# Counting edges in two spans of 24 targets for each group, where four chunks shared a span of 40

## The reference

```python
dst = jnp.minimum((1024 * jax.random.uniform(key, (32768,)) ** 2.0).astype(jnp.int32), 8191)
...
x = layernorm(x + L0(x))   # D^-1/2 (A + A^T > 0, + I) D^-1/2 (x @ W) + b
x = layernorm(x + L1(x))   # three GCN layers, edges counted with their multiplicity
x = layernorm(x + L2(x))   # attention with the mask A
x = layernorm(x + L3(x))   # two GCN layers with a ReLU between
```

## Time and profile before

| | us |
|---|---|
| median of 3 runs (lowest, highest) | 600.25 (598.95, 600.39) |
| the profiled execution, its own time | 599.57 |
| its span | 597.7 |
| TensorE busy | 582.0 |
| VectorE busy | 298.0 |
| ScalarE busy | 174.7 |
| counting stage, first to last counting matmul | 16.2 to 125.5 |

### The profile page before, as it was taken

How to read it: one execution, slowest core, us unless ns; L and a number is a source line. 1 busy time by engine, 2 the same in 40 slices (tenths; PEclk the granted TensorE clock), 3 DMA queues, 4 the chain that set the end, 5 groups by cost and what they waited for, 6 DMA issues and landing times.

```text
span 597.7 us, 6522 instructions
## 1 busy us (share of the span) xinstructions
PE 582.0 (97%) x2137; PEld 347.7 (58%) x2137; DVE 298.0 (50%) x826; ACT 174.7 (29%) x360; POOL 102.1 (17%) x112
## 2 busy tenths in 40 slices
PE   4999999999999999999999999999999999999996
PEld 3555655555787854788854544444444487458742
DVE  5999889946677314134584101333334440450065
ACT  2898688736102221011011111111114102110200
POOL 3000000006412700000142002023333170000012
PEclk9999999999999999999999999999999999999998
DMA  8514000000000000000040000000000000000012
GB/s 301 210 42 171 1 0 2 2 1 1 2 2 3 0 1 0 1 0 1 0 158 1 0 0 1 0 0 1 0 0 2 2 1 0 0 1 0 1 53 88
DMA packets 7904, 15.66 MB, mean 26 GB/s; under 512 B 432, under 2 KB 448, under 8 KB 7872
## 3 DMA queue, kind: packets, MB, share of 16 engines
q1 hardware_dynamic: 7872, 15.21, 7.0%
HBM read 13.12 MB, written 2.10 MB: 25 GB/s over the span
## 4 chain that ended last, share of the span: by engine, by line
PE 96%; DVE 1%; issue 1%; ACT 1%; DMA 0%; POOLq 0%; POOL 0%; SPq 0%; ACTq 0%
PE bank L632 18%; PE bank L587 15%; PE bank L570 15%; PE bank L737 9%; PE bank L757 9%; PE bank L499 6%; PE bank L473 5%; PE bank L725 5%; PE bank L481 2%; PE bank L444 2%; PE bank L477 2%; PE bank L463 2%; PE bank L747 1%; PE bank L436 1%; PE bank L640 1%
## 5 line engine op out<-in xcount | busy, mean ns | idle before, releaser
L384 POOL TENSOR_TENSOR rstd<-veps,mhalf 128x1 f32<-128x1 f32 x32 | 23.9, 748 | 307.0 <-DVE veps L1062 307.0
L983 DVE TENSOR_SCALAR hot_key<-col_key,keyed 128x320 bf16<-128x320 int16 x256 | 65.1, 296 | 0.1
L737 PE MATMUL bank<-xt,tt 128*128 128x512 f32 x128 | 56.1, 592 | 0.0
L757 PE MATMUL bank<-vv,probt 128*128 128x512 f32 x128 | 56.1, 592 | 0.0
L632 PE MATMUL bank<-v_sb,gt 128*128 128x512 f32 x128 | 55.3, 592 | 0.0
L587 PE MATMUL bank<-adj,y_hi 128*128 128x512 f32 x128 | 51.3, 401 | 0.0
L587 PE MATMUL bank<-adj,y_lo 128*128 128x512 f32 x128 | 50.5, 395 | 0.0
L499 PEld LDWEIGHTS bank<-hot_key,hot_lo 128*128 128x128 bf16 x256 | 25.2, 98 | 38.9 <-DVE hot_key L983 16.6
L499 PE MATMUL bank<-hot_key,hot_lo 128*128 128x320 bf16 x256 | 45.8, 302 | 0.0
L1069 DVE SCALAR_TENSOR_TENSOR xs<-bank,dinv,xs 128x512 f32<-128x512 f32 x24 | 17.7, 746 | 54.0 <-PE bank L632 38.3
L820 ACT ACTIVATE apart<-col_lo,edge_key 128x128 bf16<-128x128 int16 x128 | 43.8, 391 | 0.0
(11 more groups left out here) (178 smaller groups left out, 950.7 us busy)
## 6 DMA issues: line engine op xcount, KB each, us to landing
w_sb<-in_L_gnn_W_dram SPq DMA_DIRECT2D x3, 1024.0 KB, 5.4
xs<-in_x_dram SPq DMA_DIRECT2D x2, 1024.0 KB, 7.9
v_sb<-in_L_gnn_W_dram SPq DMA_DIRECT2D x2, 1024.0 KB, 6.7
out_dram<-xs SPq DMA_DIRECT2D x8, 256.0 KB, 2.0
w_sb<-in_L_gnn_weight_dram SPq DMA_DIRECT2D x1, 1024.0 KB, 8.2
wq_sb<-in_L_gnn_Wq_dram SPq DMA_DIRECT2D x1, 1024.0 KB, 12.1
wk_sb<-in_L_gnn_Wk_dram SPq DMA_DIRECT2D x1, 1024.0 KB, 13.8
wv_sb<-in_L_gnn_Wv_dram SPq DMA_DIRECT2D x1, 1024.0 KB, 7.5
```

Of the source, the lines that this page charges most:

```text
L737: mm = pe.matmul(bank[:, 2 * (i % 2) + c, :], tt[:, k, i * P:(i + 1) * P], xt[:, k, c * D:(c + 1) * D], start=k == 0, stop=k == FB - 1)
L757: mm = pe.matmul(bank[:, 6 + i % 2, :], probt[:, i % 2, j, :], vv[:, j, :], start=j == 0, stop=j == NB - 1)
L983: V.tensor_scalar(hot_key[:, slot * CPG + c, :], col_key[:], keyed[:, 0, bass.ds(g + c * G, 1)], None, ALU.is_equal).then_inc(hot_set, 1)
```

## The change

- WIN goes from 40 to 24, and each pair of chunks (PAIR = 2) gets a span of its own. A group has two spans, side by side in its bank. Both `hot_key` and the counting matmul go from 320 to 192 columns.
- The tables of limits, first targets and rounds are by span, so twice as long.
- A group's bank is added in two adds of 8 x 24 instead of one of 8 x 40. The first comes ahead of the one-hots of three groups later, the second behind them, with a semaphore of its own (`span_added`) between the two. Before, the one-hots came ahead of the one add.
- Places are loaded for four groups at a time, one load for each span.
- SHARE goes from 1300 to 1500 columns a group.
- The low parts of `ya` come one block earlier among the `sym`.

```diff
 CPG = 4
-WIN = 40
+WIN = 24
+PAIR = 2
 BY_DVE = 2
 EARLY = 24 * 128
-SHARE = 1300
+SHARE = 1500
...
             def chunk(at_hot, at_bank, c):
-                return pe.matmul(bank[:, at_bank, 0:KEYS], hot_lo[:, at_hot, :], hot_key[:, at_hot, :],
-                                 start=c == 0, stop=c == CPG - 1)
+                span = slice(c // PAIR * KEYS, (c // PAIR + 1) * KEYS)
+                return pe.matmul(bank[:, at_bank, span], hot_lo[:, at_hot, :], hot_key[:, at_hot, :],
+                                 start=c % PAIR == 0, stop=c % PAIR == PAIR - 1)
...
-            V.tensor_reduce(group_lim[:, 0:1], edge_rows[:, 0, :], AX.X, ALU.min)
-            then(V.tensor_reduce(group_lim[:, 1:2], edge_rows[:, 0, :], AX.X, ALU.max))
-            then(V.tensor_tensor(group_lim[:, 2:3], group_lim[:, 1:2], group_lim[:, 0:1], ALU.subtract))
+            by_span = edge_rows[:, 0, :].rearrange("g (s e) -> g s e", s=SPANS)
+            V.tensor_reduce(group_lim[:, 0, :], by_span, AX.X, ALU.min)
+            then(V.tensor_reduce(group_lim[:, 1, :], by_span, AX.X, ALU.max))
+            then(V.tensor_tensor(group_lim[:, 2, :], group_lim[:, 1, :], group_lim[:, 0, :], ALU.subtract))
...
-            def windows_at(g):
-
-                _, values = nc.values_load_multi_w_load_instructions(
-                    base_at[0:1, bass.ds(g, BODY)], engines=[mybir.EngineType.DVE], min_val=0, max_val=N,
-                    skip_runtime_bounds_check_because="the table's entries are clamped to [0, N] when it is written")
-                return values
-
-            def add_window(at_dst, seen, slot):
+            def places_at(g):
+
+                loaded = []
+                for n in range(SPANS):
+                    _, values = nc.values_load_multi_w_load_instructions(
+                        base_at[0:1, bass.ds(g + n * G, HALF)], engines=[mybir.EngineType.DVE], min_val=0, max_val=N,
+                        skip_runtime_bounds_check_because="the table's entries are clamped to [0, N] when it is written")
+                    loaded.append(values)
+                return list(zip(*loaded))
+
+            def add_span(at_dst, slot, n):
+
+                return V.tensor_tensor(count[:, :, bass.ds(at_dst, WIN)],
+                                       bank[:, slot, n * KEYS:(n + 1) * KEYS].rearrange("p (h d) -> p h d", h=NB),
+                                       count[:, :, bass.ds(at_dst, WIN)], ALU.add)
+
+            def one_group(g, at_dst, seen, slot, ahead):
 
                 dve.wait_ge(win_summed, seen + 1)
                 dve.wait_ge(win_added, seen + 2)
-                V.tensor_tensor(count[:, :, bass.ds(at_dst, WIN)],
-                                bank[:, slot, 0:KEYS].rearrange("p (h d) -> p h d", h=NB),
-                                count[:, :, bass.ds(at_dst, WIN)], ALU.add).then_inc(win_added, 1)
+                add_span(at_dst[0], slot, 0).then_inc(span_added, 1)
+                if ahead is not None:
+                    one_hots(ahead, (slot + AHEAD) % SLOTS)
+                dve.wait_ge(span_added, seen + 1)
+                add_span(at_dst[1], slot, 1).then_inc(win_added, 1)
...
-                    places = windows_at(q * BODY)
                     for n in range(BODY):
-                        one_hots(q * BODY + (n + AHEAD), (n + AHEAD) % SLOTS)
-                        add_window(places[n], r * G + q * BODY + n, n % SLOTS)
...
+                        if n % HALF == 0:
+                            places = places_at(q * BODY + n)
+                        one_group(q * BODY + n, places[n % HALF], r * G + q * BODY + n, n % SLOTS, q * BODY + (n + AHEAD))
...
-                if 3 <= h < 3 + HALF:
-                    low(h - 3, ya, xw[:, h - 3, :], dinv[:, 0, h - 3:h - 2])
+                if 2 <= h < 2 + HALF:
+                    low(h - 2, ya, xw[:, h - 2, :], dinv[:, 0, h - 2:h - 1])
```

More of the change, by code:

```diff
@@ L50, in gnn_kernel @@
     ROUNDS = (N + WIN - 1) // WIN
+    SPANS = CPG // PAIR
     KEYS = NB * WIN
     SCALE = float(D) ** -0.5
-    assert D == 512 and NB == 2 * HALF and G % BODY == 0 and BODY % SLOTS == 0 and KEYS <= 512 and G <= P
+    assert D == 512 and NB == 2 * HALF and G % BODY == 0 and BODY % SLOTS == 0 and SPANS * KEYS <= 512 and SPANS * G <= P
     with ExitStack() as ctx:
@@ L156, in gnn_kernel @@
         bqb = sb("bqb", [P, FB], F32)
[L157 to L160, removed]
+        group_lim = sb("group_lim", [G, 3, SPANS], F32)
+        group_dia = sb("group_dia", [G, 2 * SPANS, G], F32)
+        group_row = sb("group_row", [P, 2, SPANS * G], F32)
+        base_at = sb("base_at", [1, SPANS * G], I32)
         rounds_f = sb("rounds_f", [P, ROUNDS + 2], F32)
@@ L197, in gnn_kernel @@
         win_added = sem("win_added")
+        span_added = sem("span_added")
         counted = sem("counted")
@@ L487, in _ @@
             pe.wait_ge(rows_set, 1)
-            pe.matmul(bank[:, 0, 0:2 * G], ones[0:G, :], group_dia[:].rearrange("g a b -> g (a b)"),
+            pe.matmul(bank[:, 0, 0:2 * SPANS * G], ones[0:G, :], group_dia[:].rearrange("g a b -> g (a b)"),
                       start=True, stop=True).then_inc(rows_turned, 1)
@@ L947, in _ @@
             dve.wait_ge(edges_in, 32)
-            V.tensor_reduce(group_lim[:, 0:1], edge_rows[:, 0, :], AX.X, ALU.min)
-            then(V.tensor_reduce(group_lim[:, 1:2], edge_rows[:, 0, :], AX.X, ALU.max))
-            then(V.tensor_tensor(group_lim[:, 2:3], group_lim[:, 1:2], group_lim[:, 0:1], ALU.subtract))
+            by_span = edge_rows[:, 0, :].rearrange("g (s e) -> g s e", s=SPANS)
+            V.tensor_reduce(group_lim[:, 0, :], by_span, AX.X, ALU.min)
+            then(V.tensor_reduce(group_lim[:, 1, :], by_span, AX.X, ALU.max))
+            then(V.tensor_tensor(group_lim[:, 2, :], group_lim[:, 1, :], group_lim[:, 0, :], ALU.subtract))
             dve.wait_ge(const_set, 1)
-            V.tensor_scalar(group_dia[:, 0, :], ident[0:G, 0:G], group_lim[:, 0:1], None, ALU.mult)
-            V.tensor_scalar(group_dia[:, 1, :], ident[0:G, 0:G], group_lim[:, 2:3], None,
-                            ALU.mult).then_inc(rows_set, 1)
+            for n in range(2 * SPANS):
+                ins = V.tensor_scalar(group_dia[:, n, :], ident[0:G, 0:G],
+                                      group_lim[:, 2 * (n // SPANS), n % SPANS:n % SPANS + 1], None, ALU.mult)
+            ins.then_inc(rows_set, 1)
             V.tensor_scalar(bits[:, 0, :], edge_rows[:, 1, :], P - 1, None, ALU.bitwise_and)
@@ L958, in _ @@
             V.tensor_scalar(key_rows[:, 1, :], bits[:, 1, :], float(WIN), None, ALU.mult)
-            V.tensor_scalar(key_rows[:, 2, :], edge_rows[:, 0, :], group_lim[:, 0:1], None,
-                            ALU.subtract).then_inc(rows_set, 1)
+            for n in range(SPANS):
+                of_span = slice(n * PAIR * P, (n + 1) * PAIR * P)
+                ins = V.tensor_scalar(key_rows[:, 2, of_span], edge_rows[:, 0, of_span], group_lim[:, 0, n:n + 1], None,
+                                      ALU.subtract)
+            ins.then_inc(rows_set, 1)
             dve.wait_ge(rows_turned, 1)
-            then(V.tensor_copy(group_row[:].rearrange("p a g -> p (a g)"), bank[:, 0, 0:2 * G]))
+            then(V.tensor_copy(group_row[:].rearrange("p a g -> p (a g)"), bank[:, 0, 0:2 * SPANS * G]))
             then(V.tensor_reduce(rounds_f[:, ROUNDS:ROUNDS + 1], group_row[:, 1, :], AX.X, ALU.max))
@@ L1018, in _ @@
                 with dve.Fori(0, G // BODY - 1) as q:
-                    places = windows_at(q * BODY)
                     for n in range(BODY):
-                        one_hots(q * BODY + (n + AHEAD), (n + AHEAD) % SLOTS)
-                        add_window(places[n], r * G + q * BODY + n, n % SLOTS)
-                places = windows_at(G - BODY)
+                        if n % HALF == 0:
+                            places = places_at(q * BODY + n)
+                        one_group(q * BODY + n, places[n % HALF], r * G + q * BODY + n, n % SLOTS, q * BODY + (n + AHEAD))
                 for n in range(G - BODY, G):
-                    if n + AHEAD < G:
-                        one_hots(n + AHEAD, (n + AHEAD) % SLOTS)
-                    add_window(places[n - (G - BODY)], r * G + n, n % SLOTS)
+                    if n % HALF == 0:
+                        places = places_at(n)
+                    one_group(n, places[n % HALF], r * G + n, n % SLOTS, n + AHEAD if n + AHEAD < G else None)
             dve.wait_ge(win_added, rounds * G + 2)
```

## The result

The changed kernel takes 608.25 us (median of 4 runs, 607.18 to 609.1), the kernel before in the same comparison 600.32: a ratio of 1.0138, 95% interval 1.0112 to 1.0164. It is slower, as forecast, by 8 us where 11 were forecast. Two executions of the kernel before in a later comparison, of 679 and 2161 us, were in a slow state of the chip and are left out of the ratios.

What follows compares the result with a forecast made beforehand. TensorE was taken to bound the kernel before, VectorE 4% behind. Later count +16.7, given back -6.3, clock +1.0 make +11.4 us: profiled 599.57 becomes 611, median 611.5, range 601 to 618.

Steps and rivals of the forecast that it cites:

- TensorE's part: Counting matmuls of 192 columns: 0.08 us each, 14 us less; moved pieces 11 us more; counting could end at 123.
- VectorE's group: Counting stage on VectorE: 1.79 us a group, with 0.48 us from a second add's start to the next first's.
- Rival A, waits free: Counting adds: the wait costs nothing, group 1.57 us, time 598 us, or 592 with loads hidden too; chance 0.11.
- The loads: Loads of places on VectorE in counting: 0.7 us open mid-body, 1.0 at the loop's turn, 12.8 us in all.
- the lower bound that I had named: Loads of places in counting: 4 us in all if a load of four values took half as long.
- What is given back: Behind the counting: the adjacency product starts 15.6 us after the count is ready, 6.3 us earlier than before.
- The clock: Between the link turns behind the count: TensorE's clock fall costs 1 us of a possible 0 to 3.9.
- The argument from the longest gap: Between the link turns: the clock falls after some 2.5 us of nothing, and no gap there is that long.
- The sum: From 148 us on: +16.7 - 6.3 + 1.0 = +11.4 us; profiled 599.57 becomes 611, median 611.5 us.
- What was to be seen: Trace after: period 1.8 us, second-to-first add 0.48, matmuls 0.08, TensorE waiting in most groups, link at 143.
- the three signs: Wrong if second-to-first is 0.3 us, groups with loads not over 2.4 us, or product more than 18 us behind the count.

Runs made afterwards that it cites:

- the version of both sides and one load: Changed kernel with one-hots on both sides of the adds and one load of eight values in place of two of four: 595.53 us, ratio 0.9927.
- Experiment 1: Changed kernel with a group's six one-hots split, four between its two adds and two behind the second: 596.76 us, ratio 0.9951.
- experiment 5: Kernel before the change with only SHARE raised from 1300 to 1500: 604.78 us, ratio 1.0071.
- 6: Changed kernel with the table of places by group, one load of eight values in place of two of four: 606.36 us, ratio 1.0100.
- 7: Changed kernel with the low parts back at h-3, as before the change: 607.5 us, ratio 1.0139.
- 9: Changed kernel with one-hots on both sides of the adds, one load for two, and 15 unread matmuls between link turns: 592.86 us, ratio 0.9873.
- experiment 4: Changed kernel with 15 unread matmuls added between the link turns to keep TensorE busy: 604.42 us, ratio 1.0093.

## Why the prediction was right

The direction and the mechanism held, and the time lies in the range. Two of its terms did not hold in size. By its own steps:

- **TensorE's part**: 0.08 us a matmul was forecast, 0.082 measured. It was to end its counting at 123, a row of 106.3 us from 16.7 on; in the version of both sides and one load, where it is the bound, its last count is at 123.9, but the row is 108.1 us long and began at 15.8. The pieces right behind the short matmuls, 0.03 us longer each, are the larger part of the difference.
- **VectorE's group**: 1.79 us forecast, 1.80 measured; the adds at 0.357 against 0.35, the second-to-first distance 0.49 against 0.48, with the 0.13 us between them as forecast. Experiment 1 shows that it is the order: the same instructions and waits in another order are 1.57.
- **Rival A, waits free**, fell: from add to add are 0.49 us, from an add to an operation that does not wait for it 0.27. The Trainium skill says (VectorE: DVE Perf Modes, The DRAIN you can't avoid) that the semaphore after each operation costs nothing extra, as measured there on eight copies. These adds do not agree with it. Of the 0.22 us, 0.12 go to waiting for the add's end and on to the register instruction (0.35 + 0.04 for 0.27), and 0.10 to the address behind it. In the chain of keyed, where the wait is on the operation itself, only the first part is paid (0.29 + 0.04). No run has these adds with a fixed address, so the split rests on the traces alone.
- **The loads**: the term that was mis-sized. 12.8 us were forecast (0.7 x 8 + 1.0 x 7 is 12.6, a slip of 0.2), 6.8 measured: 0.22 us at each of seven places in the middle of a body, 0.88 at the first turn, 0.81 at five, and 0.33 on entering the last body. A load of four values takes 0.34 us and not 0.60 as one of eight; this was the lower bound that I had named and not taken. The eighth place in the middle hid its pair. These 6.0 us are more than the 5.4 between the forecast 143.3 and the measured 137.9; a period of 1.80 for 1.79 gives some 0.6 back. That groups with loads would be over 2.4 us was a sign named beforehand, and it failed for the seven in the middle of a body (2.02).
- **What is given back**: 6.3 us forecast, 5.6 shown by experiment 5, in which the clock fell too, and 6.1 with TensorE kept busy (22.0 against 15.9). In the change it is 3.9, as the clock took 2.2.
- **The clock**: 1 us of a possible 3.9 taken, 2.2 measured. The argument from the longest gap was wrong: no gap in the turns was as long as the 2.5 us of nothing in the earlier trace rows, the longest 1.46, and it fell all the same.
- **The sum**: +11.3 and -3.9 are 7.5 at the product, against +16.7, -6.3 and +1.0 forecast. The loads were 6 us too dear, the clock 1.2 too cheap; the two errors have opposite signs, so the sum is nearer than its terms, by luck.
- What was to be seen: period, distance and matmul as forecast; groups with pairs 2.02 and 2.61 us, where over 2.4 was forecast for all of them; TensorE late in 25 of 64 groups, where most were forecast; and the product at 18.1 us, which just passed the 18 that I had named as a sign of error. So two of the three signs came, one for the size of the loads and one for the clock term (without the fall it is 15.9).

## What to carry to other kernels

When one operation becomes two that depend on one another, look at which neighbours are left without independent work between them, across the loop's edge too: the same six operations split four and two made the count ready 11 us earlier. Look at loads into registers too: before, they stood ahead of one-hots and cost 2.2 us in all, now they stand directly ahead of an add and cost 6.8. Whether the wait of that add has a part in it is not shown; in experiment 1, whose waits are covered, the loads cost no less. And work that is moved into a stage to fill the engine that bounds it pays there at once, and comes back only as far as the stage it left was bound by it.

## What the runs showed of the hardware that was not expected

- A load of registers on VectorE takes 0.34 us for four values and 0.60 for eight.
- The granted clock fell to half without a gap as long as 2.5 us: in the 4.5 us before the fall at 147.6 TensorE had made three turns, one each 1.15 us, and stood still for the last microsecond; its longest idle time there is 1.46 us. It stayed at half for 6.8 us, through the first 3.8 us of the last unit. In four of the profiled kernels it also fell for 3.4 us about 1 to 1.5 us behind the sixteen matmuls of one row and one column (line 652 of the changed kernel, 1.94 us), while dense products ran:

```profile
177.50:180.90 3.40, 3.40 (x9) 0.50 0.00 0
```

That stretch is of the kernel with one load for two. A matmul of the product takes 0.43 us in it and 0.23 outside, so about 1.6 us are lost. It was in the profiled runs of experiments 5, 6 and 7 and, at 166 us, of 9, not in those of the others, which have the same sixteen matmuls; what brings it on is open. The runs of most kernels lie on two levels some 1.6 us apart, and the granted clock of each run partly follows them: in experiment 4 the runs with 0.998 to 0.999 took 603.7 to 604.4 us, those with 0.995 took 605.6 and 605.8. The four runs of the change, at 607.2, 607.5, 609.0 and 609.1, are not told apart by it (0.992, 0.994, 0.992, 0.992). That this fall is the difference between the levels is not shown.
- TensorE's clock rose between 12.0 and 18.2 us from kernel to kernel, with the same transposes ahead: the counting began at 15.3 us where it rose at 12.0, and at 16.2 to 16.5 where it rose at 17.7 to 18.2.
